# A gated two-branch block on one core: two expert weights loaded behind the first gather, Silu's table loaded ahead, an up product placed among the last heads, the first two down-weight splits moved

## The chip, the cores and the metric

The kernel runs on one core of one Trainium2 chip. TensorE (PE) multiplies, VectorE (DVE) and ScalarE (ACT) work element by element, GpSimd (POOL) does small work and issues the indirect transfers, and SyncE (SP) issues all other transfers. The metric is the time of one execution in microseconds (us) on the device; lower is better.

## The reference

The input `x` is 4 x 512 x 512 in f32. The first branch sends each token through one of four experts, chosen by its id; the second is a block of attention and a gated MLP, run on each of the four sequences ("batches" below).

```python
# first branch: four experts of width 512, gate, up and down all use ctx_2048[e]
hidden = layernorm(x)
expert = min(clip(ids, 0, 24999) // 6250, 3)
y[tokens of e] = (silu(hidden @ W[e].T) * (hidden @ W[e].T)) @ W[e].T
x = x + tanh(g_xattn) * y
# second branch
h0   = layernorm(x)
attn = causal_attention(rmsnorm(h0, ln1_w), Wq, Wk, Wv, Wo)       # 16 heads of 32
mod  = 0.1 * tanh(attn @ A)                                       # rank 16
h    = rmsnorm(h0, ln2_w)
gate = silu(h @ W_in.T + mod * (h @ A) @ B)                       # 2048 wide
x    = x + tanh(g_ffn) * (h0 + (gate * (h @ W_up.T)) @ W_down.T)
```

## The kernel before, in words

Every product is made from split operands: a value is rounded to a high part (ACT, `copy` into a float32r tile) and the rest is its low part (DVE, `low`), and three matmuls (high x high, low x high, high x low) stand for one. The order on each engine is written out by hand, one block per engine, and semaphores join them; so "ahead of" and "behind" below are places in that written order.

**The start.** The tokens are sorted by expert into 19 "items" of 128 rows. DVE works out the places from the ids, PE turns them into indices, and POOL gathers the rows of each item from DRAM (`gather(i)`, eight ahead in a ring). Meanwhile SP loads, in this order: ids, A, Wo, expert 0, two small ones, Wv, experts 1, 2 and 3, and the first 512 rows of `x` (`load_expert` and the lines around L266); each of the large ones is 1024 KB and a gather is 256 KB. ACT and DVE split each expert (`expert_high`, `expert_low`), and PE makes the products that fold Wv, Wo and A together (`out_products`, `value_products`).

**The items.** For item i: DVE takes the statistics of its rows (`item_stats`) and the factors of its group (`item_factors`; item 0 is a group of its own, items 1 and 2 are the next), ACT normalises (`normalise_rows`), PE turns the rows (`turn_x`), ACT and DVE split them (`x_high`, `x_low`), PE makes the first product of 12 matmuls (`first_product`), ACT takes Silu, DVE multiplies (`gated`), PE turns the result (`turn_act`) and makes the second product (`second_product`); ACT copies it out and POOL scatters it. On PE the first product of an item stands ahead of the second product of the item before.

**A batch.** First q, k and v are made, then the 16 heads, in 4 groups (q = 0..3) of 4 (j = 0..3). In `head_step` for head n PE turns the probabilities of head n+1 (`turn_probs`), makes the scores of head n+3 (`scores`), and then the product of head n with the values (`attend`). ACT has the exponentials (L936) and the high parts, DVE the maxima (L1302), part of the normalising and the low parts (L1290). In the last group there is nothing left to start ahead: `scores` comes only at j = 0, `turn_probs` up to j = 2.

**The chunks.** The MLP is 16 chunks of 128 of its 2048 columns. A chunk has 12 matmuls for the gate (`gate_product`), one for the low-rank term (`modulate`, which finishes the gate and signals `g_done`), 12 for up (`up_product`, `u_done`) and 12 for down (`down`). ACT takes Silu of the gate (L983), DVE multiplies by up (L1353), ACT and DVE split the result into `actr` and PE's `down` reads it. ACT and DVE also split the chunk's weights: gate and up two chunks ahead (`split_gate_up`, `gate_up_low`), down in the chunk's own step (L985 and `down_low`). SP's `load_chunk` loads two chunks ahead, when the split before has let the buffer go. Before, PE makes chunk 0's up product ahead of the last head's `attend` (lines 804 to 810), then after it chunk 0's gate, chunk 1's up, `modulate(0)`, chunk 1's gate, `modulate(1)` and `down` of chunk 0. The tanh of the low-rank term runs from `attend` of the last head through `att_low`, `at_sum`, `z_ok` to `zs_ok`, for which `modulate(0)` waits.

## Time and profile before

| | us |
|---|---|
| median of 3 runs | 1096.99 |
| lowest and highest | 1096.07, 1097.75 |
| the profiled execution's own time | 1097.68 |
| its span in the trace | 1095.9 |
| PE busy in it | 1047.9 (96%) |
| DVE, ACT, POOL busy | 734.6, 631.9, 176.2 |

The span begins with the first instruction and ends with the last; 1.8 us of the profiled execution's time lie outside it. PE is busy for 96% of the span, so what can be won is its idle time and the time in which it is slow. The stages are: the start up to 40 us, the items up to about 170 us, then four batches of about 232 us each, in which the heads take about 90 us and the chunks about 135 us.

### The profile page before, as it was taken

The page shows a single profiled execution, that of the slowest core. Times are in us where ns is not written, and L with a number is a line of the kernel's source. Part 1 is how long each engine was busy: PE and PEld are TensorE (multiplying, and loading weights), DVE is VectorE, ACT ScalarE, POOL GpSimd, SP SyncE. Part 2 cuts the span into 40 slices and gives each one's busy share as a digit, 9 for nine tenths or more (in the row PEclk, how much of TensorE's full clock was granted, in tenths as well). Part 3 has the DMA queues.
Part 4 walks back from the last instruction along what each step waited for, and adds up shares of the span by engine and source line. Part 5 has one row for each costly group of instructions (what it writes and reads, how often), then busy time and mean ns, then how long its engine had stood idle before and what let it go on. Part 6 is the DMA issues. An engine that isn't in the chain of part 4 may idle for free.

```text
span 1095.9 us, 18123 instructions
## 1 busy us (share of the span) xinstructions
PE 1047.9 (96%) x5400; PEld 885.8 (81%) x5401; DVE 734.6 (67%) x1662; ACT 631.9 (58%) x1477; POOL 176.2 (16%) x155
## 2 busy tenths in 40 slices
PE   5899999999999999989999999999999999899998
PEld 5787878887888888877888888878888888778887
DVE  5866748995665569975664589956655689754443
ACT  3464547885544457865544388855453588655442
POOL 4435122320000013320000023200000133200000
PEclk9999999999999999999999999999999999999999
DMA  8334133442323424342322353423234342223321
GB/s 321 100 143 163 38 116 76 93 112 87 115 86 96 145 83 119 71 137 92 112 87 86 106 150 86 111 88 113 86 101 139 90 113 66 69 88 104 97 86 48
DMA packets 47063, 115.59 MB, mean 105 GB/s; under 512 B 6800, under 2 KB 6800, under 8 KB 46096
## 3 DMA queue, kind: packets, MB, share of 16 engines
q1 hardware_dynamic: 43968, 105.06, 32.4%
q0 software_dynamic: 3040, 9.96, 2.6%
q8 instruction: 15, 0.25, 0.1%
q14 instruction: 40, 0.33, 0.1%
HBM read 76.46 MB, written 13.37 MB: 82 GB/s over the span
## 4 chain that ended last, share of the span: by engine, by line
PE 79%; DVE 9%; ACT 4%; issue 4%; DMA 2%; SPq 1%; DVEq 0%; POOL 0%; ACTq 0%; POOLq 0%
PE bank L506 62%; PE bank L708 5%; PE bank L695 5%; PE bank L677 3%; DVE wr L1290 3%; DVE nb L1302 2%; ACT big L936 2%; DMA stack<-wr 2%; PE bank L737 1%; PE bank L679 1%; DVE big L1311 1%; ACT wr L853 1%; SPq L304 1%; PE bank L562 1%; DMA big<-in_x,gidx 1%
## 5 line engine op out<-in xcount | busy, mean ns | idle before, releaser
L506 PE MATMUL bank<-hT,wr 128*128 128x512 f32 x1536 | 370.3, 391 | 0.0
L506 PEld LDWEIGHTS bank<-hT,wr 128*128 128x128 f32 x1536 | 287.8, 188 | 61.2 <-issue 1.2
L506 PE MATMUL bank<-wr,actr 128*128 128x512 f32 (+1 forms) x1224 | 301.9, 396 | 5.9 <-DVE actr L1290 3.8
L506 PEld LDWEIGHTS bank<-wr,actr 128*128 128x128 f32 x1224 | 228.1, 189 | 54.8 <-DVE actr L1290 5.6
L1340 DVE SCALAR_TENSOR_TENSOR wr<-stream,lns,wr 128x256 fp32r<-128x256 f32 x256 | 122.2, 539 | 50.8 <-ACT wr L975 50.8
L936 ACT ACTIVATE big<-bank,nb 128x512 f32<-128x512 f32 (+3 forms) x256 | 131.5, 530 | 11.5 <-DVE nb L1302 10.3
L1290 DVE TENSOR_TENSOR wr<-bank,wr 128x512 fp32r<-128x512 f32 (+1 forms) x224 | 124.7, 602 | 18.8 <-ACT wr L853 18.8
L853 ACT ACTIVATE actr<-act_sb 128x512 fp32r<-128x512 f32 x64 | 40.4, 632 | 144.2 <-DVE act_sb L1353 144.2
L853 ACT ACTIVATE wr<-bank 128x512 fp32r<-128x512 f32 (+1 forms) x224 | 102.8, 531 | 27.1 <-PE bank L506 18.7
L481 POOL TENSOR_SCALAR big<-big,rr 128x256 f32<-128x256 f32 x64 | 78.0, 1218 | 212.8 <-DVE rr L1307 212.8
L470 POOL TENSOR_TENSOR wqs<-wstage,wqs 128x1024 fp32r<-128x1024 f32 x15 | 36.1, 2408 | 460.5 <-ACT wqs L853 460.5
L1302 DVE TENSOR_REDUCE nb<-bank 128x1 f32<-128x512 f32 (+3 forms) x256 | 107.0, 477 | 3.1 <-PE bank L679 2.6
L975 ACT ACTIVATE wr<-stream,lns 128x256 fp32r<-128x256 f32 x256 | 108.4, 494 | 0.0
L983 ACT ACTIVATE sil<-bank 128x512 f32<-128x512 f32 x64 | 38.1, 596 | 119.9 <-PE bank L737 119.8
L695 PE MATMUL bank<-ident,big 128*128 128x128 f32 x640 | 86.7, 278 | 16.8 <-DVE wr L1290 16.7
L1290 DVE TENSOR_TENSOR wr<-stream,wr 128x512 fp32r<-128x512 f32 x64 | 44.2, 691 | 83.0 <-ACT wr L853 82.3
L506 PE MATMUL bank<-hT,wqs 128*128 128x512 f32 x384 | 95.8, 397 | 0.5
L695 PEld LDWEIGHTS bank<-ident,big 128*128 128x128 f32 x640 | 70.6, 141 | 30.1 <-DVE wr L1290 21.6
L708 PE MATMUL bank<-wr 128*128 128x512 f32 (+3 forms) x512 | 92.0, 322 | 0.0
L708 PEld LDWEIGHTS bank<-wr 128*128 128x128 f32 x512 | 81.3, 189 | 5.9
L677 PE MATMUL bank<-stack 96*128 96x512 f32 (+3 forms) x256 | 78.3, 369 | 6.1 <-DMA stack<-wr 3.6
L506 PEld LDWEIGHTS bank<-hT,wqs 128*128 128x128 f32 x384 | 69.8, 189 | 14.9 <-DVE wr L1290 1.7
(178 smaller groups left out, 1072.5 us busy)
## 6 DMA issues: line engine op xcount, KB each, us to landing
stream<-in_wmlp SPq DMA_DIRECT2D x64, 512.0 KB, 4.0
stack<-wr SPq DMA_DIRECT2D x192, 128.0 KB, 2.3
stream<-in_wmlp SPq DMA_DIRECT2D x64, 256.0 KB, 2.7
big<-in_x SPq DMA_DIRECT2D x4, 1024.0 KB, 5.2
big<-y_rows SPq DMA_DIRECT2D x4, 1024.0 KB, 5.8
residual<-big SPq DMA_DIRECT2D x4, 1024.0 KB, 5.7
big<-residual SPq DMA_DIRECT2D x4, 1024.0 KB, 5.7
out<-big SPq DMA_DIRECT2D x3, 1024.0 KB, 4.5
```

Source lines behind the costliest of these rows:

```text
L481: g.tensor_scalar(rows, rows, rr[:, n % 2, qt:qt + 1], None, ALU.mult).then_inc(pn_pool, 1)
L506: mm = pe.matmul(dst, lhs(pl, k), rhs(pr, k), start=start and i == 0, stop=stop and i == n - 1, skip_group_check=skip)
L677: pe.matmul(bank[bk][:, col:col + w], stack[:, par, 0, qt * P:qt * P + P], stack[:, par, 1, 0:w], start=True, stop=False, skip_group_check ...
L695: mm = pe.transpose(bank[bk][:, col + (qt - kt) * P:col + (qt - kt) * P + P], prob[par][:, src:src + P], ident[:, :])
L708: mm = pe.matmul(bank[ATT][:, kt * P:S], vst[:, kt, 64 * j:64 * j + P], pts[:, j % 2, part, at:at + w], start=False, stop=False, skip_grou ...
L853: return a.activation(dst, src, ACT.Copy)
L936: a.activation(prob[par][:, at:at + w], bank[bk][:, col:col + w], ACT.Exp, bias=nb[:, qt:qt + 1], accum_out=rs[:, par, qt:qt + 1]).then_in ...
L975: ins = a.activation(dst[:, :, dt, :], raw[:, :, dt, :], ACT.Copy, scale=lns[:, 1, dt:dt + 1])
L983: a.activation(sil[:, :], bank[GATE[par]][:, :], ACT.Silu).then_inc(g_silu, 1)
L1290: v.tensor_tensor(dst, src, high.bitcast(F32), ALU.subtract).then_inc(done, 1)
L1302: v.reduce_max(nb[:, qt:qt + 1], bank[bk][:, col:col + P * (qt + 1)], AXX, negate=True).then_inc(nb_ok, 1)
L1340: ins = v.scalar_tensor_tensor(out=dst[:, :, dt, :], in0=raw[:, :, dt, :], scalar=lns[:, 1, dt:dt + 1], in1=high[:, :, dt, :].bitcast(F32) ...
```

## The change

Five edits, in the order of the time they act in:

- SP issues experts 2 and 3 and the load of `x` only after it has waited for `row_in[0]`, the landing of the first gather; before, they stood right behind expert 1.
- ACT splits expert 1 right behind expert 0, expert 2 where expert 3 stood, and expert 3 in the item loop at i = 1. Ahead of the first item it runs a Silu on one column, and the table load of Silu stands before that.
- On PE chunk 0's up product is cut into pieces of 3, 3 and 6 matmuls that stand in `head_step` of the last group, behind `turn_probs`, at j = 0, 1 and 2. The wait on `exp_ok` moves to the gate product.
- ACT and DVE split the down weights of chunks 0 and 1 right behind the last head instead of within the chunks' own steps.
- For that the first two chunk steps are written out on ACT and, in the last batch, on DVE, and the loops start at 1.

```diff
-            for e in range(1, E):
-                load_expert(e)
+            load_expert(1)
+
+            sp.wait_ge(row_in[0], 16)
+            load_expert(2)
+            load_expert(3)
             sp.dma_start(x1, x_tiles[0]).then_inc(x1_in, 16)
...
+                if not ahead and j < QH - 1:
+                    if j == 0:
+
+                        pe.wait_ge(qk_lo, (b + 1) * (NQ * 2))
+                        pe.wait_ge(cg_hi, b * NCH + 1)
+                        pe.wait_ge(cg_lo, b * NCH + 1)
+                    up_part(0, ((0,), (1,), (2, 3))[j])
...
+            def up_part(par, tiles):
+
+                for k in tiles:
+                    for i, (pl, pr) in enumerate(PARTS):
+                        mm = pe.matmul(bank[UP[par]][:, :], wch[:, par, pl, (DT + k) * P:(DT + k) * P + P],
+                                       hT[:, pr, k, :], start=k == 0 and i == 0, stop=k == DT - 1 and i == len(PARTS) - 1,
+                                       skip_group_check=True)
+                if DT - 1 in tiles:
+                    mm.then_inc(u_done, 1)
...
                     for j in range(QH):
-                        if q == NQ - 1 and j == QH - 1:
-
-                            pe.wait_ge(qk_lo, (b + 1) * (NQ * 2))
-                            pe.wait_ge(exp_ok, (b + 1) * H * 4)
-                            pe.wait_ge(cg_hi, b * NCH + 1)
-                            pe.wait_ge(cg_lo, b * NCH + 1)
-                            up_product(0)
                         head_step(b, q, j, ahead)
 
+                pe.wait_ge(exp_ok, (b + 1) * H * 4)
                 gate_product(0)
...
             expert_high(0)
+            expert_high(1)
...
             a.activation(tg[:, :], gt[:, :], ACT.Tanh).then_inc(tanh_ok, 1)
-            expert_high(1)
-            expert_high(2)
+            act.wait_ge(const_ok, 2)
+            a.activation(warm[:, :], ones[:, 0:1], ACT.Silu).then_inc(act_own, 1)
...
                 a.activation(sil[:, :], bank[GATE[par]][:, :], ACT.Silu).then_inc(g_silu, 1)
-                act.wait_ge(cd_in[par], loads_of(b, c))
-                copy(wch[:, par, HI, CW:CW + D], stream[:, par, CW:CW + D]).then_inc(cd_hi, 1)
+                if not first:
+                    down_high(b, c, par)
                 act.wait_ge(gu_ok, n + 1)
...
                     head_step(b, NQ - 1, j, 0)
+                for par in range(2):
+                    down_high(b, par, par)
...
-            expert_high(3)
+            expert_high(2)
...
-                if i == 3:
+                if i == 1:
+                    expert_high(3)
+                elif i == 3:
...
                 quad(b, NQ - 1, 0)
+                for par in range(2):
+                    down_low(b, par, par)
...
-                    with act.Fori(0, NORM_AT) as c2:
+                    with act.Fori(1, NORM_AT) as c2:
```

On ACT at the start (`wr<-stream` and `wr<-wstage` are splits of experts, `xi` is a normalised item, `actr` a split of turned rows, `sil` Silu), before:

```order
L853 ACTIVATE bd<-bank 32x4x16 [waits woa_ok,bd_zero]
L853 ACTIVATE bd<-bank 32x4x16 x3
L875 ACTIVATE tg<-gt 128x2 [waits small_in]
L853 ACTIVATE wr<-stream 128x2048 [waits exp_in1]
L853 ACTIVATE wr<-wstage 128x2048 [waits exp_in2]
L884 ACTIVATE xi<-big,lmb,lma 128x512 [waits norm_ok]
L853 ACTIVATE actr<-bank 128x512 [waits x_turned]
L853 ACTIVATE wr<-wstage 128x2048 [waits exp_in3]
L884 ACTIVATE xi<-big,lmb,lma 128x512 [waits x_turned,norm_ok]
L897 ACT_TABLE_LOAD
L897 ACTIVATE sil<-bank 128x512 [waits h_done]
```

and with the change:

```order
L867 ACTIVATE wr<-stream 128x2048 [waits exp_in0]
L867 ACTIVATE wr<-stream 128x2048 [waits exp_in1]
L867 ACTIVATE bd<-bank 32x4x16 [waits woa_ok,bd_zero]
L867 ACTIVATE bd<-bank 32x4x16 x3
L890 ACTIVATE tg<-gt 128x2 [waits small_in]
L892 ACT_TABLE_LOAD
L892 ACTIVATE warm<-ones 128x1 [waits const_ok]
L899 ACTIVATE xi<-big,lmb,lma 128x512 [waits norm_ok]
L867 ACTIVATE actr<-bank 128x512 [waits x_turned]
L867 ACTIVATE wr<-wstage 128x2048 [waits exp_in2]
L899 ACTIVATE xi<-big,lmb,lma 128x512 [waits x_turned,norm_ok]
L912 ACTIVATE sil<-bank 128x512 [waits h_done]
```

The table load goes from ahead of the first Silu to ahead of the first `xi`, and the split that waits for `exp_in3` from behind the first `actr` to a place further down than these rows.

On PE in the last group of heads of a batch, from the end of `turn_probs` at j = 0 (`bank<-ident,big`) through the scores (`bank<-stack`), before:

```order
L695 MATMUL bank<-ident,big 128x128 [waits pt_lo]
L695 MATMUL bank<-ident,big 128x128
L673 ISA [waits stk1]
L677 MATMUL bank<-stack 128x512 [waits exp_ok]
L679 MATMUL bank<-maskr,identr 128x128
L677 MATMUL bank<-stack 128x384
```

and with the change, where `bank<-hT,wr` is the first piece of the up product:

```order
L698 MATMUL bank<-ident,big 128x128 [waits pt_lo]
L698 MATMUL bank<-ident,big 128x128
L731 REGISTER_ALU
L758 MATMUL bank<-hT,wr 128x512 [waits cg_lo,cg_hi,qk_lo]
L758 MATMUL bank<-hT,wr 128x512 x2
L676 ISA [waits stk1]
L680 MATMUL bank<-stack 128x512 [waits exp_ok]
L682 MATMUL bank<-maskr,identr 128x128
L680 MATMUL bank<-stack 128x384
```

Three matmuls and the waits for the chunk's weights and for `qk_lo` now stand between the turned probabilities and the scores of the last head.

On ACT between the last head (`wr<-bank`) and the first `down`, before:

```order
L853 ACTIVATE wr<-bank 128x256 [waits p_turned]
L1025 REGISTER_ALU
L853 ACTIVATE ysb<-bank 16x512 [waits pv_done]
L1028 ACTIVATE ysb<-act_sb 16x512 [waits at_sum]
L853 ACTIVATE zst<-sil 16x512 [waits zst_zero,z_ok]
L853 ACTIVATE zst<-sil 16x512
L1035 UNCONDITIONAL_BRANCH
L1035 ISA
L983 ACT_TABLE_LOAD
L983 ACTIVATE sil<-bank 128x512 [waits g_done]
L984 ISA
L853 ACTIVATE wr<-stream 128x512 [waits cd_in0]
L853 ACTIVATE actr<-act_sb 128x512 [waits gu_ok]
```

and with the change:

```order
L867 ACTIVATE wr<-bank 128x256 [waits p_turned]
L867 ACTIVATE wr<-stream 128x512 [waits cd_in0]
L867 ACTIVATE wr<-stream 128x512 [waits cd_in1]
L1046 REGISTER_ALU
L867 ACTIVATE ysb<-bank 16x512 [waits pv_done]
L1049 ACTIVATE ysb<-act_sb 16x512 [waits at_sum]
L867 ACTIVATE zst<-sil 16x512 [waits zst_zero,z_ok]
L867 ACTIVATE zst<-sil 16x512
L1002 ACT_TABLE_LOAD
L1002 ACTIVATE sil<-bank 128x512 [waits g_done]
L867 ACTIVATE actr<-act_sb 128x512 [waits gu_ok]
```

The two splits of down weights (`wr<-stream`) now stand ahead of the wait for `pv_done`, and nothing stands between Silu and the split of its product.

## Rows read from the trace of the kernel before

**Rows 1.** The page: TensorE's busy row in section 1, its granted clock in 40 slices.
```profile
PE 1047.9 (96%) x5400; PEld 885.8 (81%) x5401; DVE 734.6 (67%) x1662; ACT 631.9 (58%) x1477; POOL 176.2 (16%) x155
...
PEclk9999999999999999999999999999999999999999
```

**Rows 2.** Chain that ended last, start to first full-speed product: start us, us, what.
```profile
16.95 7.87 DMA big<-in_x,gidx
...
24.84 0.69 DVE sti L1237
...
31.72 1.19 DVE sti L1237 x2
...
35.88 0.81 ACT xi L884
...
36.71 0.42 ACT L897
...
38.00 0.61 ACT sil L897
...
40.18 3.00 PE bank L506 x12
```

**Rows 3.** Timeline, a gather at the start and a load with a gather behind it.
```profile
21.70 0.95 POOL L421 DMA_INDIRECT big<-in_x,gidx  x1 [0.30 <-issue]
...
50.94 0.35 SPq L274 DMA_DIRECT2D wstage<-in_wqk  x1
...
51.20 1.01 POOL L421 DMA_INDIRECT big<-in_x,gidx  x1 [0.15 <-issue]
```

**Rows 4.** Issue to landing (us, last): gathers of 36.95, 90.19, 51.20; the 50.94 load.
```profile
big<-in_x,gidx POOLq DMA_INDIRECT x1, 3.4
...
big<-in_x,gidx POOLq DMA_INDIRECT x1, 7.4
...
big<-in_x,gidx POOLq DMA_INDIRECT x1, 8.2
...
wstage<-in_wqk SPq DMA_DIRECT2D x1, 2048.0 KB, 8.3
```

**Rows 5.** Timeline of PE, first turned item, first product, products folded behind it.
```profile
29.25 1.11 PE L562 MATMUL bank<-ident,xi 128*128 128x128 f32 x4 [4.67 <-ACT xi L884]
...
31.86 5.20 PE L506 MATMUL bank<-wr,actr 128*128 128x512 f32 x12
36.90 1.00 PE L528 MATMUL bank<-bd,big 128*128 128x64 f32 x8
```

**Rows 6.** Timeline of ACT, a split of an expert and the first copy of `ysb`.
```profile
30.89 1.90 ACT L853 ACTIVATE wr<-wstage 128x2048 fp32r<-128x2048 f32 x1
...
46.41 0.60 ACT L853 ACTIVATE ysb<-bank 128x512 f32<-128x512 f32 x1 [2.10 <-PE bank L506]
```

**Rows 7.** Stretch 24 to 25 us: PE, PEld, DVE, ACT, POOL, PEclk, DMA share, GB/s.
```profile
24.00:25.00 1.00, 0.58 (x3) 0.39 (x2) 0.16 (x1) 0.61 (x1) 0.80 (x1) 1.00 1.05 227
```

**Rows 8.** Batch 0, last heads: two rows of PE's timeline, then one of the chain.
```profile
247.69 0.50 PE L677 MATMUL bank<-stack 96*128 96x512 f32 x1 [0.58 <-ACT big L936]
251.16 1.04 PE L695 MATMUL bank<-ident,big 128*128 128x128 f32 x6 [0.88 <-DVE wr L1290]
...
256.54 2.80 PE bank L506 x12
```

**Rows 9.** Waits of PE, whole run: us in total, times, longest us.
```profile
PE bank L506 <- DVE actr L1290: 3.8, 4, 1.0
...
PE bank L677 <- ACT big L936: 2.4, 4, 0.7
```

**Rows 10.** Batch 0, chain from chunk 0's gate to its down product.
```profile
266.85 0.63 ACT wr L853
...
268.11 0.69 DVE act_sb L1353
...
270.24 0.98 PE bank L506 x3
```

More of the change, by code:

```diff
@@ L976, in split_gate_up, with down_high, chunk_step @@
                 ins.then_inc(cg_hi, 1)
-            def chunk_step(b, c, par, more=True):
+            def down_high(b, c, par):
+                act.wait_ge(cd_in[par], loads_of(b, c))
+                copy(wch[:, par, HI, CW:CW + D], stream[:, par, CW:CW + D]).then_inc(cd_hi, 1)
+            def chunk_step(b, c, par, more=True, first=False):
                 n = b * NCH + c
@@ L1033, in batch @@
                 copy(zst[64:64 + R, :], zrow).then_inc(zs_hi, 1)
+                for par in range(2):
+                    chunk_step(b, par, par, first=True)
                 if more:
-                    with act.Fori(0, NORM_AT) as c2:
+                    with act.Fori(1, NORM_AT) as c2:
                         for par in range(2):
@@ L1046, in batch @@
                 else:
-                    with act.Fori(0, NCH // 2 - 1) as c2:
+                    with act.Fori(1, NCH // 2 - 1) as c2:
                         for par in range(2):
@@ L1346, in down_low, with chunk_step @@
                 low(wch[:, par, LO, CW:CW + D], stream[:, par, CW:CW + D], wch[:, par, HI, CW:CW + D], cd_lo)
-            def chunk_step(b, c, par, more=True):
+            def chunk_step(b, c, par, more=True, first=False):
                 n = b * NCH + c
-                down_low(b, c, par)
+                if not first:
+                    down_low(b, c, par)
                 dve.wait_ge(g_silu, n + 1)
@@ L1440, in batch @@
                 quad(b, NQ - 1, 0)
+                for par in range(2):
+                    down_low(b, par, par)
                 dve.wait_ge(at_low, b + 1)
@@ L1448, in batch @@
                 low(zst[32:32 + R, :], zrow, zst[0:R, :], zs_ok)
+                for par in range(2):
+                    chunk_step(b, par, par, first=True)
                 if more:
-                    for par in range(2):
-                        chunk_step(b, par, par)
                     with dve.Fori(1, 1 + TT // 2) as c2:
@@ L1467, in batch @@
                 else:
-                    with dve.Fori(0, NCH // 2 - 1) as c2:
+                    with dve.Fori(1, NCH // 2 - 1) as c2:
                         for par in range(2):
```

## The prediction, on record before the changed kernel ran

> **What bounds the kernel now.** I read the page first, then the chain that ended last, then what PE waits for, then the timelines around its gaps. The page has PE busy for 1047.9 of 1095.9 us [rows 1], so some 48 us of idle time can be won, and beside it only time in which PE is slow. The chain shows that in the middle of a chunk stage PE works without a gap; what lies elsewhere is at three places that this change touches.
>
> First the start. The first gather is issued at 16.95 and lands 7.87 us later, and the statistics of item 0 begin at 24.84 [rows 2]. A gather that meets no loads lands in 3.4 us [rows 4]. So the first rows are some 4 us late. From there the chain goes through items 1 and 2: their statistics (31.72), their factors, the normalised item 1 (35.88), then 36.71 to 38.00 for Silu's table, Silu at 38.00, and the second first-product at 40.18 [rows 2]. From there on the items run at PE's own pace.
>
> Second the last heads of a batch. PE is idle for 0.58 us before the last scores, since they wait for the exponentials of the head before, and for 0.88 us before the next turned probabilities [rows 8]. The first of the two comes in each of the four batches, 2.4 us in total [rows 9].
>
> Third the first down product of a batch: 0.95 us of idle time in each batch, 3.8 in total, longest 1.0, behind DVE's split of `actr` [rows 9]. The chain shows why: ACT splits the down weights at 266.85, DVE after it, and only at 268.11 does DVE multiply gate and up [rows 10].
>
> **The start, part by part.** The first gather loses the 3 MB that stood ahead of it. Its issue takes 0.2 us longer than a usual one, so I take 3.6 us, landing at 20.55 instead of 24.82: item 0 moves ahead by 4.3 us, and with it expert 1's low split behind its factors and the first product, from 31.86 to 27.6 [rows 5]. [...] I leave it at 5.20, so it ends at 32.8.
>
> What is late next are items 1 and 2, which share one set of factors, so the later of their gathers decides. That one is issued at 21.70 [rows 3]. SP now issues its three loads at about 20.6 to 22.1, just before and beside it. The trace has two such cases: a gather at 51.20, behind a load of 2048 KB at 50.94 [rows 3], landed after 8.2 us and that load after 8.3 [rows 4]; and one at 90.19, behind the loads of a stage change, landed after 7.4 [rows 4]. I take 7.8, the middle: landing at 29.5. Its statistics take half of 1.19, to 30.1. In the trace they end at 32.91 and the product follows at 40.18, 7.27 later; 1.29 of it is the table load (36.71 to 38.00) [rows 2], which now runs while ACT waits for the first rows. That leaves 5.98: the second first-product starts at 36.1 instead of 40.2. **Gain 4.1 us.** The first product doesn't stand in the way: ending at 32.8, it would allow 32.8 + 2.2 (38.00 to 40.18) = 35.0, which is the upper bound, a gain of 5.2. The lower bound: the gather lands with the last of 3 MB, and 2 MB took 8.3, so 12.4 from 20.6, at 33.0; then the product starts at 39.6. By then PE has been idle from 33.8 (the folded products behind the first one take 1.00 [rows 5]) to 37.4, nearly as long as the 4.67 before the slow product, and twelve matmuls at 5.20 instead of 3.00 cost 2.2. Together a loss of 1.6.
>
> [...]
>
> The split of expert 3 moves to i = 1 on ACT. It takes 1.90 us and ACT stands idle for 2.10 there, ahead of the first copy of `ysb` [rows 6]. All of that stretch moves with the product, so it fits with 0.2 to spare: nothing. If its load came later than some 42 us it would hold up the copy and the split behind it; I have it near 29 to 33. Expert 1's split on ACT falls while ACT waits for `woa_ok`: nothing. POOL issues the same gathers; DVE's order at the start is unchanged. The load of B and that of `x` come about 6 us later and are wanted tens of us after.
>
> **The last heads.** The first piece has 3 of 12 matmuls that took 2.80 [rows 8], so 0.70 us. It starts when the probabilities are turned and fills the 0.58; the scores come 0.12 later. DVE, which takes their maxima, is by then still normalising, and the gap of 0.88 behind them has room. So the turned probabilities at 251.16 stay where they are. The other pieces (0.70 and 1.40) stand where PE had no gap and are only moved ahead of `attend`; the splits of the last head, which were hidden by the whole product, get the last piece and one `attend` (1.40 + 1.2) instead. So 0.70 us a batch, **2.8 us**. Bounds: 2.4, if only the idle time that was there is filled, to 2.8; nothing, if the shift of the scores came back in full at the next wait and the small pieces held up the splits.
>
> **The first down product.** With the down weights split behind the last head, on engines that then wait for `attend`, the multiply no longer waits for 266.85 to 268.11 [rows 10]: it follows Silu's end, 1.1 us earlier. PE's own work up to `modulate(1)` then ends last, 0.95 after which it now starts. **0.95 x 4 = 3.8 us**, with 0.2 to spare. That reserve is thin: if half of it and some more is lost, 3.0. The same edit frees the buffers earlier, so SP loads chunk 3 earlier; nobody on the path waits for it. SP's queue holds nothing behind it that is wanted sooner. Loops written out drop three table loads of Silu a batch, all beside a busy PE: nothing.
>
> **Sum.** 4.1 + 2.8 + 3.8 = 10.7 us. Against the profiled execution's own 1097.68 that is 1087.0. The median of the runs shown is 0.7 lower, so 1086.3 is my time.
>
> **Rivals.**
> - The gathers do not wait behind the loads. For it speaks that the queues are different ones; against it both cases in rows 4. Then the start gives its bound of 5.2: 5.2 + 2.8 + 3.8 = 11.8, time 1085.2. [...]
> - Items 1 and 2 come with the last load and PE falls back to the lower clock: the start gives its lower bound, and with the middle of their bounds for the others -1.6 + 2.6 + 3.4 = 4.4, time 1092.6. For it speaks that 3 MB stand ahead, not 2; against it, that the gather at 90.19, behind five loads of a stage change, landed sooner than the one behind a single load of 2 MB [rows 4].
> - The pieces do not do what they are placed for: the waits of the last heads are chains of ACT and DVE, and the shift comes back. Then 4.1 + 0 + 3.8 = 7.9, time 1089.1.
> - Slower than before: items 1 and 2 starve. In the stretch in which loads and gathers last ran together the core moved 227 GB/s [rows 7]. If all of 3 loads and 3 gathers (3.9 MB) went at that rate from 21.9 on, about a us after the first is issued, the later gather lands at 39.1, the product starts at 45.7 and runs slow: 5.5 + 2.2 lost against 6.6 won, 1.1 us slower, 1098.1. It decides against the change from a landing of about 38 us on. Against it speaks that one gather never took more than 8.2 of all those in rows 4, and this would be 17.
>
> **How the numbers follow.** The forecast has 0.60, the gathers that don't wait 0.14, the late items 0.14, the pieces without effect 0.07, the starved items 0.02; 0.03 are for what I do not see. The range of 8 in 10 reaches from 1084.5 (the second case, less half a us of spread between runs) to 1092.0, which takes in the forecast, the first and third rival and the earlier half of the late items. A difference of 0.2% (2.2 us) is about what a measurement of this kernel can tell from no change. All cases but the starved one are faster by more; I give part of the late and of the unseen ones to no change: 0.93 faster, 0.05 same, 0.02 slower.
>
> **What would show it.** In the chain: the first gather landing near 20.5; statistics of items 1 and 2 ending near 30; no table load before the first Silu; the second first-product near 36. In PE's waits: the row of 2.4 us behind the exponentials gone or at 0, the row of 3.8 behind `actr` gone. The distance from one batch's start to the next shorter by 1.65 us. I am wrong if the later gather lands after 32 or before 28, if the PE gap before the second product exceeds 2 us, if a new wait stands in front of `attend` of the last head, or if the copy of `ysb` at i = 1 is late.

## Result and the profile after

| | us |
|---|---|
| changed kernel, median of 4 runs (lowest to highest) | 1086.86 (1086.08 to 1088.3) |
| before, 4 runs beside it | 1097.33 (1096.07 to 1097.75) |
| ratio, with its 95% interval | 0.9913 (0.9901 to 0.9925) |
| profiled execution, its span | 1088.3, 1086.6 |

The changed kernel is 10.5 us faster. The forecast was 1086.3 with a range of 1084.5 to 1092.0, so the time lies in it and 0.6 us off. The terms behind it do not agree as well: one was too large and two were too small.

The page of the changed kernel, against [rows 1]. TensorE's busy time is 0.6 longer than before while the span is 9.3 shorter: it is idle time that went. One slice, near 885 us, shows a lower granted clock (8 tenths); before had none.

```profile
PE 1048.5 (96%) x5400; PEld 887.1 (82%) x5401; DVE 736.0 (68%) x1662; ACT 612.9 (56%) x1463; POOL 177.4 (16%) x155
...
PEclk9999999999999999999999999999999989999999
```

**The start**, in the chain of the changed kernel (start us, us, what), answers to [rows 2]:

```profile
21.69 7.64 DMA big<-in_x,gidx
...
29.36 0.69 DVE sti L1262
...
30.37 0.51 DVE nm L1272
...
30.90 0.54 DVE nmi L1274
...
33.60 0.17 DVE lmb L1283
...
33.80 0.82 ACT xi L899
...
34.67 0.67 PE bank L565 x4
...
36.94 2.99 PE bank L509 x12
```

The first gather is off the chain, and so is the table load. What decides is the gather issued at 21.69, as forecast. The second first-product starts at 36.94 instead of 40.18: 3.2 us where 4.1 were forecast.

**The last heads** of batch 0, in the chain, answer to [rows 8]. L698 are the turned probabilities, L758 the pieces of the up product, L711 `attend`, L509 gate, up and down products.

```profile
249.20 0.69 PE bank L758 x3
249.89 1.21 PE bank L711 x8
251.10 1.11 PE bank L698 x10
252.22 1.39 PE bank L758 x6
253.61 2.48 PE bank L711 x16
256.09 5.53 PE bank L509 x24
...
261.85 2.73 PE bank L509 x12
...
264.83 5.74 PE bank L509 x24
```

The chain from the first piece on names PE alone. The last line is 24 matmuls without a break: the gate of chunk 1 and, behind `modulate(1)` of chunk 0, the down product follow with no wait on ACT or DVE, where the chain of before had Silu, two splits of weights and the multiply ([rows 10] shows one of the splits and the multiply).

**PE's waits**, whole run (us in total, times, longest us). Both rows of [rows 9] are gone:

```profile
PE bank L698 <- DVE wr L1315: 16.8, 28, 1.0
...
PE bank L680 <- DMA stack<-wr: 3.0, 6, 1.0
...
PE bank L565 <- ACT xi L899: 2.1, 3, 1.3
```

**Where the 9.3 us of span are.** Each batch begins with the first transfer into `stack` and its chunks begin with the gate of chunk 0; from these two starts in the chains of both kernels:

| stretch, us | before | after | gain |
|---|---|---|---|
| start and items, to the first `stack` | 171.37 | 167.99 | 3.38 |
| heads, four batches | 89.18, 89.15, 89.18, 90.69 | 88.10, 88.14, 88.17, 92.25 | 1.08, 1.01, 1.01, -1.56 |
| chunks, four batches (the last to the end) | 143.25, 143.22, 143.22, 136.64 | 142.09, 142.14, 142.07, 135.65 | 1.16, 1.08, 1.15, 0.99 |

Where starts of the other kernels are given below they are read in the same way.

### The profile page after: what moved, and what is told of

The parts are those of the page before. It is cut to its first block, busy times and chain, and to the rows that moved or that the text cites. A ratio compares the mean times of both kernels' runs of the same rounds, so it can differ in the third digit from the quotient of the medians.

```text
span 1086.6 us, 18076 instructions
## 1 busy us (share of the span) xinstructions
PE 1048.5 (96%) x5400; PEld 887.1 (82%) x5401; DVE 736.0 (68%) x1662; ACT 612.9 (56%) x1463; POOL 177.4 (16%) x155
## 4 chain that ended last, share of the span: by engine, by line
PE 81%; DVE 9%; issue 3%; ACT 3%; DMA 2%; SPq 1%; POOL 1%; DVEq 0%; ACTq 0%; POOLq 0%
PE bank L509 62%; PE bank L711 5%; PE bank L698 5%; PE bank L680 3%; DVE wr L1315 3%; DVE nb L1327 2%; ACT big L951 2%; PE bank L747 1%; DMA stack<-wr 1%; DVE big L1336 1%; PE bank L682 1%; ACT wr L867 1%; SPq L307 1%; PE bank L758 1%; PE bank L565 1%
## 5 line engine op out<-in xcount | busy, mean ns | idle before, releaser
L509 PE MATMUL bank<-hT,wr 128*128 128x512 f32 x1488 | 358.4, 390 | 0.0
L509 PEld LDWEIGHTS bank<-hT,wr 128*128 128x128 f32 x1488 | 278.9, 188 | 59.9 <-issue 1.3
L509 PE MATMUL bank<-wr,actr 128*128 128x512 f32 (+1 forms) x1224 | 301.4, 396 | 2.3 <-DVE actr L1297 1.5
L509 PEld LDWEIGHTS bank<-wr,actr 128*128 128x128 f32 x1224 | 227.7, 189 | 50.5 <-issue 3.2
L951 ACT ACTIVATE big<-bank,nb 128x512 f32<-128x512 f32 (+3 forms) x256 | 131.5, 530 | 11.5 <-DVE nb L1327 10.5
L698 PE MATMUL bank<-ident,big 128*128 128x128 f32 x640 | 86.1, 277 | 16.8 <-DVE wr L1315 16.8
L509 PE MATMUL bank<-hT,wqs 128*128 128x512 f32 x384 | 96.9, 400 | 0.5
L698 PEld LDWEIGHTS bank<-ident,big 128*128 128x128 f32 x640 | 70.7, 141 | 29.1 <-DVE wr L1315 21.2
L711 PE MATMUL bank<-wr 128*128 128x512 f32 (+3 forms) x512 | 91.9, 323 | 0.0
L711 PEld LDWEIGHTS bank<-wr 128*128 128x128 f32 x512 | 82.2, 191 | 6.4
L1379 DVE TENSOR_TENSOR act_sb<-bank,sil 128x512 f32<-128x512 f32 x64 | 44.2, 691 | 58.3 <-PE bank L509 51.6
L509 PEld LDWEIGHTS bank<-hT,wqs 128*128 128x128 f32 x384 | 70.6, 190 | 15.2 <-DVE wr L1315 1.7
```

The lines of the kernel that those rows point to most:

```text
L509: mm = pe.matmul(dst, lhs(pl, k), rhs(pr, k), start=start and i == 0, stop=stop and i == n - 1, skip_group_check=skip)
L698: mm = pe.transpose(bank[bk][:, col + (qt - kt) * P:col + (qt - kt) * P + P], prob[par][:, src:src + P], ident[:, :])
L711: mm = pe.matmul(bank[ATT][:, kt * P:S], vst[:, kt, 64 * j:64 * j + P], pts[:, j % 2, part, at:at + w], start=False, stop=False, skip_grou ...
L951: a.activation(prob[par][:, at:at + w], bank[bk][:, col:col + w], ACT.Exp, bias=nb[:, qt:qt + 1], accum_out=rs[:, par, qt:qt + 1]).then_in ...
L1379: v.tensor_tensor(act_sb[:, :], bank[UP[par]][:, :], sil[:, :], ALU.mult).then_inc(gu_ok, 1)
```

## Experiments

The theory was the forecast's sum: start 4.1, heads 2.8, down product 3.8, independent of each other, with gathers that wait behind loads. Its rivals were gathers that don't wait, pieces without effect, and a start that has its gain from something else. The first three kernels each make one part of the change alone; medians are given with lowest and highest, and the ratio to before with its interval.

### The three parts alone

Only the edits of the start:

```diff
-            for e in range(1, E):
-                load_expert(e)
+            load_expert(1)
+
+            sp.wait_ge(row_in[0], 16)
+            load_expert(2)
+            load_expert(3)
...
+            expert_high(1)
...
-            expert_high(1)
-            expert_high(2)
+            act.wait_ge(const_ok, 2)
+            a.activation(warm[:, :], ones[:, 0:1], ACT.Silu).then_inc(act_own, 1)
...
-            expert_high(3)
+            expert_high(2)
...
-                if i == 3:
+                if i == 1:
+                    expert_high(3)
+                elif i == 3:
```

> The kernel before with the edits of the start alone (SP's wait for the first gather, the moved expert splits on ACT, the Silu ahead). My theory, from the trace of the changed kernel: the second first-product starts at 36.9 us instead of 40.2, and nothing of that is given back, so 3.3 us are gained, about 1094. Rival: the items' second stall near 90 us or the first batch absorbs some of it; then less than 2 us remain at the end of the span.

Measured: 1095.21 (1094.34 to 1098.23), ratio 0.9985 (0.9971 to 0.9999); before was 1096.88 beside it. That is 1.7 us (0.1 to 3.2 by the interval), not the 4.1 of the forecast nor the 3.3 expected here. The second first-product starts where it does in the whole change, 3.2 us earlier than before, but takes 4.58 instead of 2.99 us. Nothing more is lost behind it: the first `stack` transfer still comes 1.9 us earlier (169.48 for 171.37), so the rival's small number came true, but not by its mechanism. PE's timeline of this kernel:

```profile
36.97 4.58 PE L509 MATMUL bank<-wr,actr 128*128 128x512 f32 x12 [0.41 <-DVE actr L1269]
```

Only the pieces of the up product:

```diff
+                if not ahead and j < QH - 1:
+                    if j == 0:
+
+                        pe.wait_ge(qk_lo, (b + 1) * (NQ * 2))
+                        pe.wait_ge(cg_hi, b * NCH + 1)
+                        pe.wait_ge(cg_lo, b * NCH + 1)
+                    up_part(0, ((0,), (1,), (2, 3))[j])
...
-                            up_product(0)
...
+                pe.wait_ge(exp_ok, (b + 1) * H * 4)
```

> The kernel before with only the up product in pieces. The predicted term was 0.70 us a batch, 2.8 in all. My theory now: 1.0 a batch in the first three (0.7 of filled idle time and 0.35 of a wait inside the turned probabilities of the last head, which the piece ahead of them covers), and 3 to 4 us over all. Rival: the 0.35 comes from the down splits being elsewhere, not from the pieces; then it is 0.7 a batch here. The chain has to show ten transposes of the last head in 1.1 us instead of 1.47.

Measured: 1092.16 (1091.36 to 1094.93), ratio 0.996 (0.9947 to 0.9972): 4.7 us. The heads of batches 0 to 2 take 88.11, 88.14 and 88.14, as in the whole change, so their gain is the pieces' own and not that of the moved splits. It is 1.01 to 1.07 a batch, not 0.70.

Only the moved splits of down weights, with the loops that this needs:

```diff
+                for par in range(2):
+                    down_high(b, par, par)
...
+                for par in range(2):
+                    chunk_step(b, par, par, first=True)
...
-                    with act.Fori(0, NORM_AT) as c2:
+                    with act.Fori(1, NORM_AT) as c2:
...
+                for par in range(2):
+                    down_low(b, par, par)
```

> The kernel before with only the first two down splits moved and the loops begun at 1. My theory: 0.95 a batch for the gap before the first down product and 0.15 for the wait behind it, 1.1 a batch, 4.4 in all, about 1092.9. Rival: the table loads of Silu that go with the written-out loop carry part of it; then the gap before the first down product is more than 0 and the gain differs between the last batch, where six loads go, and the others, where three go.

Measured: 1091.61 (1091.22 to 1093.25), ratio 0.9955 (0.9938 to 0.9973): 5.3 us. The stretches of chunks take 142.14, 142.11, 142.13 and 135.61, as in the whole change: 1.1 a batch and 4.3 in all. Of PE's waits, the one for the exponentials is still there and the one of 3.8 behind `actr` is gone; what is left for `actr` is a single one, in the items:

```profile
PE bank L677 <- ACT big L936: 2.4, 4, 0.7
...
PE bank L506 <- DVE actr L1280: 1.5, 1, 1.5
```

In the last batch six table loads of Silu go instead of three, and the gain of its chunks is not larger (1.03 against 1.09 to 1.11 in the others). So these table loads beside a busy PE, 1.28 us each, carried nothing, as forecast.

The starts of these two kernels are as before, yet the first `stack` transfer comes at 170.09 (pieces only) and 170.69 (splits only) against 171.37 in the profile of before. DVE's timeline of the kernel with the pieces only, the statistics of item 0:

```profile
23.39 0.69 DVE L1248 BATCH_NORM_STATS2 sti<-big 128x6 f32<-128x512 f32 x1 [2.81 <-DMA big<-in_x,gidx]
```

In the other kernel they begin at 24.18, and before at 24.84 [rows 2]. The three kernels have the same instructions up to there. So the landing of the first gather behind 3 MB of loads differs from one execution to the next, and the one profiled before was the latest of three.

### Without the table load ahead

The changed kernel less two lines:

```diff
-            act.wait_ge(const_ok, 2)
-            a.activation(warm[:, :], ones[:, 0:1], ACT.Silu).then_inc(act_own, 1)
```

> The changed kernel without the Silu ahead of the first item, so that its table is loaded where it was. The prediction had the load as 1.3 us of the path. Rival, from the trace of the changed kernel: there the path to the second first-product went from the normalised item 1 through its turned rows and their splits, and Silu and the gated product ran beside it, so that the load would cost less than its length. Theory: the second first-product starts 1.3 us later than 36.9. Rival: 0.6 to 1.0 later.

Measured: 1087.85 (1087.31 to 1088.88), ratio 0.9916 (0.9898 to 0.9933). Its timelines of ACT and PE:

```profile
34.64 1.28 ACT L910 ACT_TABLE_LOAD   x1
```

```profile
38.11 5.11 PE L509 MATMUL bank<-wr,actr 128*128 128x512 f32 x12
```

The second first-product starts 1.17 us later than in the changed kernel's profile, where 1.29 had been taken for the table load. That part of the start's term holds; the rival's 0.6 to 1.0 is short of it. The medians differ by 1.0, which by itself is within their spread.

### How much a gather waits behind loads

Four kernels issue different amounts beside the gathers of items 1 and 2. The first lets all three rows land ahead of any load:

```diff
-            sp.wait_ge(row_in[0], 16)
+            for k in range(3):
+                sp.wait_ge(row_in[k], 16)
             load_expert(2)
             load_expert(3)
```

> The changed kernel, but SP waits for the first three gathers before it issues experts 2 and 3 and x: no load stands beside the gathers of items 1 and 2. Theory (gathers wait behind loads): the later of the two lands 3.5 us after its issue at 21.7, at 25.2, not at 29.3; then expert 2, issued at 25.2, lands near 30.5 and its split on ACT holds up the normalised item 1; the second first-product starts at 35.5 instead of 36.9. Rival (the gathers are slow among themselves): it still lands at 27 or later with no load beside it.

The second lets one load of 1 MB go behind the first gather, and the others behind the third:

```diff
             sp.wait_ge(row_in[0], 16)
             load_expert(2)
+            for k in (1, 2):
+                sp.wait_ge(row_in[k], 16)
             load_expert(3)
             sp.dma_start(x1, x_tiles[0]).then_inc(x1_in, 16)
```

> The changed kernel, but SP issues only expert 2 behind the first gather, and expert 3 and x behind the third. Theory (gathers wait for what was issued before them): with 1 MB in place of 3 the later gather lands near 26.5, the first product is then what ends last, and the second starts near 34.9; with no gap on PE it runs at the higher clock. Rival (a gather is served at a fixed delay as soon as any load is beside it): it lands at 29.3 as before.

The third lets two go:

```diff
             sp.wait_ge(row_in[0], 16)
             load_expert(2)
             load_expert(3)
+            for k in (1, 2):
+                sp.wait_ge(row_in[k], 16)
             sp.dma_start(x1, x_tiles[0]).then_inc(x1_in, 16)
```

> The changed kernel, but the load of x waits for the first three gathers: 2 MB stand beside the later gather of items 1 and 2. Measured so far: 3.6 us from issue to landing with none, 5.0 with 1 MB, 7.6 to 8.8 with 3 MB. Theory (it waits for what was issued before it): 6.8 to 7.6, since expert 3 is issued about 0.9 before the gather and x about 0.3. Rival (the second and third load no longer matter, only the first): 5 to 5.5.

The fourth is the changed kernel itself, run again:

> The changed kernel once more, for a second profile of it. Theory: with three loads beside the gathers PE stands idle for 1 to 2 us before the turned rows of item 1, and in most executions its granted clock then falls, so the second first-product takes 4.3 to 5.1 us instead of 3.0; the heads of the last batch take 88.5 to 89.6 us, not the 92.3 of the first profile. Rival: the first profile was typical; product 3.0, last heads 92.

| loads beside it | kernel | gather of 21.7, issue to landing | second first-product | median (lowest to highest) | ratio |
|---|---|---|---|---|---|
| none | all rows first | 3.6 | 36.54, 2.97 | 1084.09 (1083.35 to 1087.06) | 0.9885 (0.9856 to 0.9914) |
| one | one load | 5.0 | 35.67, 3.01 | 1083.74 (1083.43 to 1084.27) | 0.9876 (0.9852 to 0.99) |
| two | two loads | 8.4 | 37.62, 4.99 | 1090.8 (one run) | |
| three | the change | 7.6 | 36.94, 2.99 | 1086.86 (1086.08 to 1088.3) | 0.9913 (0.9901 to 0.9925) |
| three | the change again | 8.0 | 37.23, 4.35 | 1087.24 (1085.51 to 1088.13) | 0.9915 (0.9898 to 0.9931) |

The landings are the trace's own where it gives them; for two loads and for the change again they are the start of the statistics less the issue at 21.69. In all six profiles with three loads this gather took 7.6 to 8.0 us; the 8.8 in the expectation above is the gather of item 1, issued before it. The landing rows of this gather (us from issue to landing, last), first of the change, then of the kernel with one load, then with all rows first:

```profile
big<-in_x,gidx POOLq DMA_INDIRECT x1, 7.6
```

```profile
big<-in_x,gidx POOLq DMA_INDIRECT x1, 5.0
```

```profile
big<-in_x,gidx POOLq DMA_INDIRECT x1, 3.6
```

DVE's timeline of the kernel with two loads and of that with one, the statistics behind that landing:

```profile
30.13 0.69 DVE L1264 BATCH_NORM_STATS2 sti<-big 128x6 f32<-128x512 f32 x1 [2.04 <-DMA big<-in_x,gidx]
```

```profile
27.41 1.28 DVE L1264 BATCH_NORM_STATS2 sti<-big 128x6 f32<-128x512 f32 x2
```

So the gather does wait: 1.4 us for the first load beside it, 4 to 5 for two or three. The gather of item 1, issued at 18.4, goes the same way: 5.4 us with no load, 7.7 with one, 9.4 in the change. That the gathers don't wait is ruled out. Two loads, in the one profile there is, cost as much as three, which was not expected; the third is the one of `x`, issued at 21.39, about when this gather is (21.69). Behind 2 MB the landing took more than twice as long as with no load, 8.4 us against 3.6. By what rule the queues share the DMA engines no run shows.

With all rows first the gather is in early and the product still starts at 36.54, 1.0 later than expected, since ACT stands with expert 2's split ahead of item 1, and that load came at 31.6, not at 30.5:

```profile
31.60 1.91 ACT L868 ACTIVATE wr<-wstage 128x2048 fp32r<-128x2048 f32 x1 [4.83 <-DMA wstage<-in_wexp]
```

Ordering the loads is thus a trade in these runs: with three of them early the rows land after 7.6 to 8.0 us instead of 3.6, with all of them late ACT waits 4.83 us for the load that it splits. One load is the best of the amounts tried, by start (35.67, expected 34.9); its median does not differ from that of all rows first.

**The clock.** Most kernels with three loads, and the one with two, show a slow second first-product. PE's timelines of the change again and of the kernel with one load:

```profile
34.96 0.66 PE L565 MATMUL bank<-ident,xi 128*128 128x128 f32 x4 [2.42 <-ACT xi L899]
...
37.23 4.35 PE L509 MATMUL bank<-wr,actr 128*128 128x512 f32 x12 [0.41 <-DVE actr L1288]
```

```profile
35.67 3.01 PE L511 MATMUL bank<-wr,actr 128*128 128x512 f32 x12 [0.70 <-DVE actr L1290]
```

The same two in the stretch 36 to 40 us (us, then PE, PEld, DVE, ACT, POOL busy, granted clock, DMA share, GB/s), and in front of them the change's first profile:

```profile
36.00:40.00 4.00, 3.59 (x19) 2.84 (x20) 4.00 (x5) 1.34 (x3) 1.57 (x1) 1.00 0.40 125
```

```profile
36.00:40.00 4.00, 3.43 (x11) 2.64 (x12) 3.83 (x5) 1.55 (x3) 1.70 (x2) 0.59 0.33 112
```

```profile
36.00:40.00 4.00, 4.00 (x21) 3.30 (x20) 4.00 (x6) 1.59 (x4) 1.86 (x1) 1.00 1.03 276
```

Of six profiles with three loads five show a granted clock of 0.50 to 0.67 there and the product at 4.28 to 5.11 us; only the first of the changed kernel shows 1.00, with 2.99. The kernel with two loads is at 0.50, with 4.99. In the kernels with one load, with all rows first and with both edits (below) it is 1.00 and the product takes 2.97 to 3.01. In the profiles with the lower clock the product is thus 1.3 to 2.1 us longer.

How long PE was idle ahead of item 1's turned rows does not sort these profiles. It was 2.42 us in the change again, 2.12, 1.88 and 1.61 in three others with a fall, but only 0.80 in the kernel with the filled wait (below), where the clock fell too. In the change's first profile it was 1.28 and with all rows first 1.01, and there the clock held. PE's timelines of these three, in this order:

```profile
34.62 0.66 PE L565 MATMUL bank<-ident,xi 128*128 128x128 f32 x4 [0.80 <-ACT xi L901]
...
36.89 4.28 PE L509 MATMUL bank<-wr,actr 128*128 128x512 f32 x12 [0.28 <-DVE actr L1290]
```

```profile
34.67 0.66 PE L565 MATMUL bank<-ident,xi 128*128 128x128 f32 x4 [1.28 <-ACT xi L899]
```

```profile
34.27 0.66 PE L566 MATMUL bank<-ident,xi 128*128 128x128 f32 x4 [1.01 <-ACT xi L900]
```

So why the clock falls in one and not in the other is open. How often it falls can be seen without profiles, in the mean granted clock of each execution: it was below 1.000 in 28 of the 30 executions with three loads (the change, run twice, start only, without the table load ahead, late pieces, filled wait), and in 1 of the 12 with one load, with all rows first or with both edits. (The mean does not say where it fell.) Of the change again the one execution at 1.000 took 1085.51 us, the three at 0.997 took 1086.88 to 1088.13.

For one load this accounts for the gain: the product starts 1.3 us earlier and is 1.3 to 2.1 shorter in most executions, 2.6 to 3.4 together, and the medians are 3.1 apart. The shorter product, which comes with the clock at 1.00, is about half of that or more.

Of what was expected of the change again, the slow product came (4.35), but the last heads took 90.42 us, not 88.5 to 89.6.

### The pieces, otherwise placed

All pieces but the first at j = 2, so that only the first fills a gap of PE:

```diff
-                    up_part(0, ((0,), (1,), (2, 3))[j])
+                    up_part(0, ((0,), (), (1, 2, 3))[j])
```

> The changed kernel with the pieces 3, 0 and 9 instead of 3, 3 and 6, so that no piece stands ahead of the last turned probabilities. Theory: the 0.35 us a batch beyond the filled gap come from the piece that gives the splits time: the ten transposes take 1.47 again and the heads 88.5 us instead of 88.1. Rival: it makes no difference where the pieces stand; 88.1.

Measured: 1088.34 (1086.72 to 1089.64), ratio 0.9916 (0.9889 to 0.9943). The heads take 88.53, 88.50 and 88.50 in batches 0 to 2, 0.4 longer than in the change, and the chain has the ten turned probabilities behind the missing piece at 1.46 instead of 1.11:

```profile
251.13 1.22 PE bank L711 x8
252.35 1.46 PE bank L698 x10
253.81 2.08 PE bank L758 x9
```

The chain of before has the same length for them:

```profile
253.86 1.46 PE bank L695 x10
```

This is the 0.35 us that the forecast lacked. In the kernel with the pieces only it is gone too (1.11), so it is not due to the moved splits. The account that fits: with PE there earlier, the last turned probabilities have a wait for the low parts inside them (`turn_probs` waits for `pt_lo` between its transposes), and the piece at j = 1 puts them later and fills that wait as well. The rows show the length and what changes it; the wait itself they do not list. The medians do not resolve it (1.1 to 1.5 apart, with ranges that overlap); the stretches of the traces do.

One piece goes ahead of the turned probabilities, where PE waits for DVE once a batch:

```diff
+                if not ahead and j == 1:
+                    up_part(0, (1,))
...
-                    up_part(0, ((0,), (1,), (2, 3))[j])
+                    up_part(0, ((0,), (2,), (3,))[j])
```

> The changed kernel with four pieces of three matmuls: the second stands ahead of the turned probabilities of head 14 at j = 1, in the gap of 0.88 us that the chain of exponentials, maxima and low parts leaves there; the third and fourth at j = 1 and 2. Theory: that gap is free time on PE, so 0.7 us more a batch, less up to 0.35 because the wait inside the last turned probabilities comes back: the heads take 87.4 to 87.8 us instead of 88.1, and 1.4 to 2.8 us over all. Rival: with less work between the last turned probabilities and the last attend, PE waits there for the splits; then nothing is won.

Measured: 1083.77 (1083.62 to 1085.94), ratio 0.9882 (0.9856 to 0.9908), about 3 us faster than the change by the medians, though the intervals just overlap. The wait that it fills falls from 16.8 us to 13.5, in PE's waits of this kernel:

```profile
PE bank L698 <- DVE wr L1317: 13.5, 26, 1.0
```

The heads take 87.53, 87.50 and 87.51, 0.6 less than in the change; the 0.35 does not come back (the last turned probabilities take 1.12). Four times 0.6 is 2.4; the rest of the 3 us can be the last batch, where this profile has heads of 88.29 and those of the change 92.25 and 90.42.

### Both

The change with the one load and the filled wait together:

> The changed kernel with one load beside the gathers and with the four pieces among the last heads. Theory: the two act at different places and add up: second first-product at 35.7 and at the higher clock, heads 87.5 us a batch, 0.6 a batch below one load alone, so about 1081.5. Rival: the piece in the gap of the heads or the later load of x takes it back; 1083.5 as with either alone.

Measured: 1080.16 (1080.11 to 1081.16), ratio 0.9855 (0.9839 to 0.9872). The second first-product starts at 35.56 and takes 2.97, the first `stack` transfer comes at 166.54. The heads of batches 0 to 2 take 87.42, 87.47 and 87.45, 0.7 less than with one load alone (88.15, 88.15 and 88.17). The two edits gave 3.1 and 3.1 alone (from 1086.86) and give 6.7 together: within their spread they add. This version is 16 us faster than before.

## Why the prediction was right, and where it was not

**Start, 4.1 forecast, about 1.5 measured.** This is the term that was mis-sized most, though its mechanism held: the first gather landed 3.6 us after its issue, as taken; the later gather at 29.33, forecast 29.5; the table load gave 1.17 of 1.29; the copy of `ysb` at i = 1 was not late (43.17, behind a wait of 0.32 for PE). Three things were missing.

- The step "in the trace they end at 32.91 and the product follows at 40.18" took the factors at their old duration. In the changed kernel from the end of the statistics (30.05) to that of the factors (33.77) it is 3.72 us, before 2.94. Three small operations of 128 x 2 took about 0.5 us instead of 0.17 (two of them stand in the chain above), while POOL issued a gather and filled a tile of 128 x 512. That is 0.8, and the gain of this profile is 3.2 (40.18 to 36.94). The timelines of DVE and of POOL in the changed kernel:

```profile
30.37 0.50 DVE L1272 TENSOR_SCALAR nm<-mvi 128x2 f32<-128x2 f32 x1
30.90 0.54 DVE L1274 TENSOR_SCALAR nmi<-nm 128x2 int32<-128x2 int32 x1
30.98 0.47 DVE L1275 TENSOR_SCALAR nm<-nm 128x2 f32<-128x2 f32 x1
```

```profile
29.93 0.95 POOL L424 DMA_INDIRECT big<-in_x,gidx  x1 [0.30 <-issue]
30.88 0.54 POOL L443 MEMSET apad<- 128x512 f32 x1
```

  The slow operations end when POOL's do, at 30.88 and 31.42, to 0.03 us.
- The forecast gave the lower clock only to the case of late gathers. It came (0.50 to 0.67) in five of six profiles with gathers that landed in time, and the product was 1.3 to 2.1 us longer with it. The idle time of over 2 us ahead of the second product, which was named as a sign of being wrong, came as well: not in the first profile (1.28), but in the change again (2.42). For the first product, which was left at 5.20, no row shows a lower clock: [rows 1] has 9 in every slice, and it took 4.93 and 4.07 us in the two profiles of the change, with 1.00 shown. What makes it slow stays open. So that the 5.20 goes with the lower clock, as the second rival has it, was my own estimate and was not shown.
- The base was one execution, whose first gather was late. Over the three kernels with the old start the first `stack` transfer comes at 171.37, 170.09 and 170.69, mean 170.7; over five with the new one (the change twice, start only, late pieces, filled wait) at 167.99, 169.54, 169.48, 169.84 and 169.16, mean 169.2. The difference is 1.5, and the kernel with the start alone was 1.7 faster.

The lower bound of -1.6 and the range covered this; the value taken did not.

**Last heads, 2.8 forecast, 3.1 measured in three batches, 4.1 if the fourth does as they do.** The 0.70 for the first piece was right (0.69 in the chain) and the wait for the exponentials is gone. What it left out is the 0.35 a batch in the last turned probabilities: the gain is 1.01 to 1.08 in each of batches 0 to 2. The fourth can't be read from one profile: its heads took 92.25 in the change's first profile and 90.42 in the second, 88.92 with the pieces alone. Over the profiles in which the granted clock held there, four kernels with the pieces of the change took 88.4 to 89.5 us, mean 88.9, and three without them 89.6 to 90.7, mean 90.0, which speaks for about 1 there too. The statement that "the turned probabilities at 251.16 stay where they are" is where this was missed: I looked only at the gap ahead of them.

**First down product, 3.8 forecast, 4.4 measured.** The wait of 0.95 is gone, and the multiply no longer stands in the chain. The other 0.15 to 0.2 in each of batches 0 to 2 lie in the stretch of the chunks too and come with the moved splits alone as well; which wait they are was not traced. The reserve of 0.2 held. From one batch's start to the next it is 230.19 and 230.28 us instead of 232.43 and 232.37: 2.1 to 2.2 shorter, forecast 1.65.

**Sum.** With the fourth batch's heads taken as the others, 1.5 + 4.1 + 4.4 = 10.0, against 10.5 measured between medians and 8.8 in the second comparison (1096.08 less 1087.24). The medians of the three parts alone, 1.7, 4.7 and 5.3, make 11.7; each has a spread of 1 us or more. The first profile alone has 3.4, 1.5 and 4.4, the 9.3 us of its span. So the forecast was right in its total because a start that was 2.6 too large and 1.9 too little elsewhere nearly cancelled. The mechanisms named were right; that the total came within 0.6 us was luck.

**Rivals.** Gathers that don't wait: ruled out, 3.6 against 5.0 and 7.6 to 8.4. Items 1 and 2 late, with a slow product: the gathers were in time, but the clock's half of it came true in five of six profiles (0.50 to 0.67). Pieces without effect: ruled out by the pieces alone. Starved items: the gather that decides took at most 8.4 us, far from the 17 that it needed, and the core moved 403 GB/s at 24 to 28 us where the rival had taken 227.

## What to carry over

A gather that the critical path waits for landed here after 3.6 us with no load beside it, after 5.0 with 1 MB and after 7.6 to 8.4 with more, and the earliest start of the second first-product (35.67 us, 35.56 with both edits) came with one 1 MB load behind the first gather and the rest behind the third. But a load must not come later than its consumer's place in its engine's order allows: with all rows first ACT waited 4.83 us for it, and the product started at 36.54. Work without dependencies that is cut into pieces filled several waits of PE here: the 0.58 us before the last scores, and with the filled wait 0.6 a batch more. A group of instructions that grows with no wait listed (1.46 us against 1.11) counts too. A stretch that depends on DMA landings should be sized from several executions: here the profile of before had its first `stack` transfer 0.7 us later than the mean of three. The same goes for TensorE's granted clock: the first profile of the change has 1.00 at 36 to 40 us, where the five others with three loads have 0.50 to 0.67 and a product 1.3 to 2.1 us longer.

## What was not expected of the hardware

- Two loads of 1 MB hold up a gather of 256 KB as long as three do (8.4 us in the one profile with two, 7.6 to 8.0 with three; 5.0 with one, 3.6 with none). Why it levels off is open.
- TensorE's granted clock fell to 0.50 to 0.67 at 36 to 40 us in six profiles, with idle times ahead of item 1's turned rows from 0.80 to 2.42 us, and stayed at 1.00 in two with 1.01 and 1.28 us. The second of these is a profile of the change itself, of which another profile shows the fall.
- In the heads of the last batch a fall came in both profiles of the change and in that with two loads (0.50, 0.67 and 0.62 at 884 to 888 us), after waits of 1.05, 0.80 and 0.97 us for the `stack` transfer. In the kernel with late pieces the same wait was 1.09 us, and the clock held at 1.00. The change's first profile:

```profile
884.00:888.00 4.00, 4.00 (x13) 3.42 (x13) 3.30 (x9) 1.99 (x9) 1.23 (x1) 0.50 0.43 98
```

In it PE's timeline has the product of six matmuls at 2.73 us, and at the same place of the batch before at 1.60:

```profile
886.11 2.73 PE L509 MATMUL bank<-hT,wqs 128*128 128x512 f32 x6
```

```profile
652.89 1.60 PE L509 MATMUL bank<-hT,wqs 128*128 128x512 f32 x6
```

The heads of the last batch took 90.4 to 92.3 us in the three profiles with the fall and 88.3 to 90.7 in the others, where before has the 90.7. Whether the clock accounts for all of that was not tried and stays open.
- DVE's TENSOR_SCALAR operations on 128 x 2 elements took up to 0.72 us instead of 0.17 while POOL was at work. In the ten profiles with the new start every one of them that took 0.3 us or more ends within 0.04 us of the end of a gather's issue or of the fill on POOL, wherever it starts. With one load the factors come earlier and meet another of POOL's operations, and again the two ends coincide (29.63), in the timelines of DVE and POOL:

```profile
29.20 0.43 DVE L1276 TENSOR_SCALAR nmi<-nm 128x2 int32<-128x2 int32 x1
```

```profile
28.69 0.94 POOL L426 DMA_INDIRECT big<-in_x,gidx  x1 [0.30 <-issue]
```

  That the ends coincide is thus read from many rows. That DVE waits for POOL there is my reading of them and was not shown: no run took POOL's work away. The gathers' issues and the fill can stand elsewhere in POOL's order, which would be the experiment.
